# Layer output of a two-layer cross-attention kernel: from four groups of rows to two halves of dimensions, turned back to rows at the layer's end

## The reference, cut to what matters

```python
B, Q, D, H, K, T, F = 8, 56, 256, 16, 128, 1500, 1024
for i in (1, 2):                                   # two layers, both read the same ctx
    h  = layer_norm(x, ln_scale[i], ln_offset[i])
    qh = (h @ wq[i] + bq[i]).reshape(B, Q, H, K)
    kh = (ctx @ wk[i] + bk[i]).reshape(B, T, H, K)  # plus one bias key per head
    vh = (ctx @ wv[i] + bv[i]).reshape(B, T, H, K)  # plus one bias value per head
    weights = softmax(einsum('bqhk,bthk->bhqt', qh, kh) / sqrt(K))
    c  = einsum('bhqt,bthk->bqhk', weights, vh).reshape(B, Q, H * K)
    x  = x + c @ wo[i] + bo[i]                      # "layer output" below
h   = layer_norm(x, ln_mlp_scale, ln_mlp_offset)
out = x + gelu(h @ w_fc1 + b_fc1) @ w_fc2 + b_fc2
```

## Time and profile before

| what | us |
|---|---|
| median of three runs (lowest, highest) | 1249.38 (1248.67, 1249.79) |
| the profiled execution, its own time | 1248.49 |
| its span, first to last instruction | 1246.7 |
| TensorE matmuls busy | 1220.7 (98%) |
| TensorE weight loads busy | 1123.9 (90%) |
| GpSimd busy | 890.2 (71%) |
| VectorE, ScalarE busy | 783.0, 780.1 (63% each) |
| mean granted TensorE clock, share of full speed | 0.999 |

### The profile page before, as it was taken

How to read it: one execution, slowest core, us unless ns; L and a number is a source line. 1 busy time by engine, 2 the same in 40 slices (tenths; PEclk the granted TensorE clock), 3 DMA queues, 4 the chain that set the end, 5 groups by cost and what they waited for, 6 DMA issues and landing times. The chain is left out here.

```text
span 1246.7 us, 26766 instructions
## 1 busy us (share of the span) xinstructions
PE 1220.7 (98%) x7896; PEld 1123.9 (90%) x7896; DVE 783.0 (63%) x1295; ACT 780.1 (63%) x1495; POOL 890.2 (71%) x744
## 2 busy tenths in 40 slices
PE   7999999999999999999999999999999999999998
PEld 6779999999999999998887999999999999999897
DVE  6755666565656565666754666666666666666754
ACT  5756666666666565676584666666666666667665
POOL 4747777777777777678641878686868687866882
PEclk9999999999999999999999999999999999999999
DMA  5401222222222222223320122222222222222321
GB/s 173 130 18 51 56 74 57 71 58 70 61 67 63 66 66 62 57 64 91 110 68 18 38 60 68 62 68 62 67 62 66 63 66 64 65 52 61 74 89 41
DMA packets 147720, 83.60 MB, mean 67 GB/s; under 512 B 121116, under 2 KB 122540, under 8 KB 147672
## 3 DMA queue, kind: packets, MB, share of 16 engines
q1 hardware_dynamic: 147128, 82.27, 25.0%
q10 hardware_dynamic: 544, 0.75, 0.2%
HBM read 68.56 MB, written 0.53 MB: 55 GB/s over the span
## 5 line engine op out<-in xcount | busy, mean ns | idle before, releaser
L602 POOL TENSOR_TENSOR pt<-slots,pt 125x512 fp32r<-125x512 f32 (+3 forms) x384 | 449.5, 1176 | 189.9 <-ACT slots L1067 167.4
L777 PE MATMUL psum<-qs,ctx 128*125 128x384 f32 (+1 forms) x2304 | 534.8, 368 | 1.3 <-ACT slots L1093 0.8
L777 PEld LDWEIGHTS psum<-qs,ctx 128*125 128x125 f32 x2304 | 394.8, 186 | 47.4 <-ACT slots L1093 8.4
L798 PE MATMUL psum<-ctx,pt 125*128 125x258 f32 (+1 forms) x1344 | 385.0, 286 | 5.4 <-ACT on L1074 4.4
L799 PE MATMUL psum<-ctx,pt 125*128 125x256 f32 (+1 forms) x1344 | 379.3, 282 | 0.0
L800 PE MATMUL psum<-ctx,pt 125*128 125x258 f32 (+1 forms) x1344 | 378.6, 282 | 0.0
L1066 ACT ACTIVATE pt<-slots 125x512 fp32r<-125x512 f32 (+3 forms) x384 | 221.6, 577 | 195.6 <-DVE slots L1351 163.6
L1363 DVE TENSOR_TENSOR t_max<-psum,t_max 125x512 f32<-125x512 f32 (+1 forms) x320 | 199.4, 623 | 230.0 <-PE psum L777 230.0
L1093 ACT ACTIVATE slots<-psum 125x512 f32<-125x512 f32 (+1 forms) x384 | 207.5, 541 | 157.6 <-DVE t_max L1363 147.0
L798 PEld LDWEIGHTS psum<-ctx,pt 125*128 125x128 f32 (+1 forms) x1344 | 253.4, 189 | 22.7 <-issue 8.1
L799 PEld LDWEIGHTS psum<-ctx,pt 125*128 125x128 f32 (+1 forms) x1344 | 254.2, 189 | 5.8
(11 more groups left out here) (101 smaller groups left out, 974.4 us busy)
## 6 DMA issues: line engine op xcount, KB each, us to landing
nat_stage<-ctx_nat SPq DMA_DIRECT2D x60, 375.0 KB
tr_stage<-ctx_tr SPq DMA_DIRECT2D x60, 375.0 KB, 3.1
w_raw<-weights SPq DMA_DIRECT2D x70, 256.0 KB, 2.7
qt<-turn SPq DMA_DIRECT2D x256, 32.0 KB, 2.0
qt<-turn SPq DMA_DIRECT2D x224, 24.0 KB, 1.9
dk_rest<-dk_rows SPq DMA_DIRECT2D x2, 768.0 KB, 5.6
w_raw<-weights ACTq DMA_DIRECT2D x2, 256.0 KB, 5.3
dk_first<-dk_rows SPq DMA_DIRECT2D x2, 256.0 KB, 4.2
```

The lines of the kernel that those rows point to most:

```text
L602: nc.gpsimd.tensor_tensor(split_weights(h, LO, c), logits(h, c), as_f32(split_weights(h, HI, c)), ALU.subtract).then_inc(pt_lo, 1)
L777: last = mm(scores(h, k), ctx_tr_chunk(half, a, c), qs[h][:, m, half, 0:R], start=(half, a, m) == terms[0], stop=(half, a, m) == terms[-1])
L798: mm(out_bank[:, 0:D + 2], hi, ctx_nat_hi(c), start=(c == 0), stop=False, skip_group_check=True)
```

## The change

The output of a layer is now accumulated with the dimensions on the partitions: two banks (`YT_BANK`: half 0 in bank 6, half 1 in bank 5), each 128 dimensions x 448 rows. The operands change sides: 128 columns of the output weights are the weights of the array, and `cs` moves, all 448 columns at once. A head takes 2 halves x 3 terms = 6 matmuls. The residual is put there by eight products. At the layer's end half 0 is copied to `ht32` by ScalarE and half 1 by VectorE, TensorE turns both back to rows in `Y_BANK` with eight transposes, and the statistics start from there. Three more filler products stand before the transposes. The MLP keeps the old form.

```diff
@@ tensor @@
             def residual(m):
                 pe.wait_ge(xb_ready, INIT + m * RG + RG)
-                for g in range(RG):
-                    mm(Y_BANK[g][0:RGP, 0:D], ident[0:RGP, 0:RGP], xres[:, g, :], start=True, stop=False)
+                for half in range(DC):
+                    for g in range(RG):
+                        mm(YT_BANK[half][:, g * RGP:(g + 1) * RGP], xres[:, g, half * P:(half + 1) * P],
+                           ident[0:RGP, 0:RGP], start=(g == 0), stop=False)
...
+            def output_half(u, half, last_head):
+                for a, m in TERMS:
+                    last = mm(YT_BANK[half][:, 0:ROWS], w[u][:, m, D + half * P:D + (half + 1) * P], cs[u][:, a, :],
+                              start=False, stop=last_head and (a, m) == (LO, HI))
+                return last
+            def output_cols(u, n):
+                pe.wait_ge(c_lo, INIT + n + 1)
+                for half in range(DC):
+                    last = output_half(u, half, False)
+                last.then_inc(w_used, 1)
+            def last_output_cols(n):
+                pe.wait_ge(c_lo, INIT + n + 1)
+                for half in range(DC):
+                    output_half(2, half, False)
+                pe.wait_ge(c_lo, INIT + n + 2)
+                output_half(3, 0, True).then_inc(yt_mm, 1)
+                output_half(3, 1, True).then_inc(w_used, 2)
+            def turn_back(l):
+                def turned(g, half):
+                    return nc.tensor.transpose(Y_BANK[g][0:RGP, half * P:(half + 1) * P],
+                                               ht32[:, half, g * RGP:(g + 1) * RGP], ident[:])
+                pe.wait_ge(yt_act, INIT + l + 1)
+                for g in range(RG - 1):
+                    turned(g, 0)
+                pe.wait_ge(yt_dve, INIT + l + 1)
+                for g in range(RG - 1):
+                    turned(g, 1).then_inc(rows_mm, 1)
+                turned(RG - 1, 0)
+                turned(RG - 1, 1).then_inc(rows_mm, 1)
...
                 output_quad(heads + 4 * (QUADS - 1), jobs + 4 * (QUADS - 1), True, False, True)
+                keep_busy(3)
+                turn_back(l)
                 keep_busy(15)
                 norm_transposes(l + 1)
@@ scalar @@
                 output_quad(QUADS - 1, False, True)
+                act.wait_ge(yt_mm, INIT + l + 1)
+                go(ht32[:, 0, :], YT_BANK[0][:, 0:ROWS], ACT.Copy).then_inc(yt_act, 1)
                 for g in range(RG):
                     act.wait_ge(xn_ready, INIT + (l + 1) * RG + g + 1)
@@ vector @@
             def output_statistics(m, jobs):
+                dve.wait_ge(w_used, INIT + jobs)
+                V.tensor_copy(ht32[:, 1, :], YT_BANK[1][:, 0:ROWS]).then_inc(yt_dve, 1)
                 for g in range(RG):
-                    rows_complete(m - 1, jobs, g)
+                    dve.wait_ge(rows_mm, INIT + (m - 1) * RG + g + 1)
                     statistics(m, g)
```

More of the change, by code:

```diff
@@ L210, in build @@
         C_BANK = [bank[0], bank[1], bank[7], bank[2]]
+        YT_BANK = [bank[6], bank[5]]
         Y_BANK = [bank[3], bank[4], bank[6], bank[5]]
@@ L248, in build @@
         c_mm, c_hi, c_lo, g32_ready = sem("c_mm"), sem("c_hi"), sem("c_lo"), sem("g32_ready")
-        y_mm, xb_ready, saved, x_ready = sem("y_mm"), sem("xb_ready"), sem("saved"), sem("x_ready")
+        y_mm, yt_mm, yt_act, yt_dve, rows_mm = (
+            sem("y_mm"), sem("yt_mm"), sem("yt_act"), sem("yt_dve"), sem("rows_mm"))
+        xb_ready, saved, x_ready = sem("xb_ready"), sem("saved"), sem("x_ready")
         out_written = sem("out_written")
@@ L260, in build @@
         started_by = {
-            "pe": [w_used, xt_mm, q_mm, qp_mm, lb_mm, s_mm, mt_mm, nb_mm, pv_mm, ot_mm, pn_picked, c_mm, y_mm],
-            "act": [saved, w_hi, h_hi, q_hi, qp_out, most_qs_hi, first_qs_hi, copied, exp_done, on_act, ot_out,
+            "pe": [w_used, xt_mm, q_mm, qp_mm, lb_mm, s_mm, mt_mm, nb_mm, pv_mm, ot_mm, pn_picked, c_mm, y_mm, yt_mm, rows_mm],
+            "act": [saved, yt_act, w_hi, h_hi, q_hi, qp_out, most_qs_hi, first_qs_hi, copied, exp_done, on_act, ot_out,
                     p80_hi, oth_early, oth_hi, c_hi, g32_ready],
@@ L265, in build @@
                     dv_ready, gp_ready, gp_used, q_lo, first_qs_lo, lb_rows_ready, nat_hi, tr_hi, max_done,
-                    max_ready, sub_done, rden_ready, pn_ready, on_dve, ot_last, turned, moved, p80_lo,
+                    max_ready, sub_done, rden_ready, pn_ready, on_dve, yt_dve, ot_last, turned, moved, p80_lo,
                     oth_lo, c_lo, xb_ready],
@@ L871, in output_quad @@
                     if extra and first and u == 0:
-                        output_rows(0, n, False)
+                        output_cols(0, n)
                         head_context(2, n + 2, job + 2, True)
@@ L875, in output_quad @@
                         head_context((u + 2) % 4, n + (u + 2), job + (u + 2), extra)
-                        output_rows(u, n + u, first and u == 0)
-                if last_quad:
+                        if extra:
+                            output_cols(u, n + u)
+                        else:
+                            output_rows(u, n + u, first and u == 0)
+                if last_quad and extra:
+                    last_output_cols(n + 2)
+                elif last_quad:
                     last_output_rows(n + 2)
@@ L1239, in tr_part_hi, with rows_complete @@
                 V.tensor_copy(hi_part, tr_stage[:]).then_inc(tr_hi, 1)
-            def rows_complete(n, jobs, g):
+            def rows_complete(jobs, g):
                 if g < RG - 1:
-                    dve.wait_ge(y_mm, INIT + n * (RG - 1) + g + 1)
+                    dve.wait_ge(y_mm, INIT + g + 1)
                 else:
@@ L1260, in output_sum @@
                 for g in range(RG):
-                    rows_complete(LAYERS, LAYERS * JOBS + FT, g)
+                    rows_complete(LAYERS * JOBS + FT, g)
                     V.tensor_tensor(xres[:, g, :], Y_BANK[g][0:RGP, 0:D], xres[:, g, :], ALU.add).then_inc(x_ready, 1)
```

## The result

The changed kernel takes 1252.32 us (median of nine runs, 1250.15 to 1255.81), the kernel before 1248.67 us beside it (nine runs, 1245.10 to 1249.79). The ratio is 1.0035, with a 95% interval of 1.0024 to 1.0046, so 3.0 to 5.7 us slower. In a second series, with six runs of the changed kernel and 26 of the kernel before, it was 1.0043 (1.0026 to 1.0060). The forecast was +5.05 us, slower.

What follows compares the result with a forecast made beforehand. From head 6 GpSimd and VectorE, not TensorE, were taken to set the output stage's pace. +6.09 (turning back) - 1.16 (last outputs) + 0.12 (residual) - 0 (other outputs) = +5.05 us, on 1249.38 giving 1254.4 us; range 1251.0 to 1256.4.

Steps and rivals of the forecast that it cites:

- Outputs of heads 0 to 12: Output stage: 0.21 us less TensorE time per head, hidden by waiting for GpSimd's weight tile; taken as 0.
- Turns of 2.99 us: Output stage from head 6: `pm`, `oth` and weight tile alternate on GpSimd and VectorE, 2.99 us per head.
- all of it: Upper bound for the earlier outputs: every head's 0.21 us is gained, 2.5 us per layer.
- rival of TensorE's pace: Output stage: TensorE sets the pace, so every output gives its 0.21 us; +0.05 us, 1249.4 us, chance 0.08.
- The last outputs: Last three heads' outputs, with no context between: 36 matmuls become 18, -0.58 us per layer, -1.16 us in all.
- E: The end of a layer's last output matmul, from which the forecast counted the layer's end.
- The residual: Residual put into the output banks: 8 instructions become 16 of 112 columns, +0.06 us per layer, +0.12 us in all.
- Turning back: Layer's end: copies, transposes and unoverlapped statistics delay `ln_v` to E + 4.26, +3.54 and +2.55 us, +6.09 us in all.
- Sum: Whole kernel: all parts together, +5.05 us, slower.
- turning back is cheaper: Rival, layer's end: ScalarE's copy not behind the weight tiles, `ln_v` at E + 3.2; 2.1 us less, 1252.3 us, chance 0.12.
- The clock: Rival, layer's end: idle TensorE is granted 1.2 GHz until the next stage; 1.5 us per layer more, 1257.4 us, chance 0.05.
- The unlocking: Rival, output stage: `oth` precedes `pm`, tile runs alone, 2.64 us per head; total -2.0 us, 1247.4 us, chance 0.05.

Runs made afterwards that it cites:

- extra_matmul: Changed kernel with one more 448-column matmul, its result unread, in the outputs of heads 0 to 13; 1253.36 us, ratio 1.0039 to the kernel before.
- copy_first: Changed kernel with ScalarE's copy of half 0 ahead of its last two weight tiles; 1250.69 us, ratio 1.0016 to the kernel before.
- no_turn_back: Changed kernel without the two copies, three fillers and transposes, so results are wrong; 1249.93 us, ratio 1.0011 to the kernel before.
- pm_on_act_after: Changed kernel with the masked bias product `pm` made by ScalarE instead of GpSimd; 1248.53 us, ratio 1.0000 to the kernel before.
- tile_first_after: Changed kernel with `pm` on ScalarE, half 0 copied before its last two weight tiles, `pm` and tile before `oth`; 1239.09 us, ratio 0.9937.

## Why the prediction was right, step by step

- *Outputs of heads 0 to 12 give nothing.* Right. Turns of 2.99 us in both kernels; extra_matmul put 0.2 us per head back and lost nothing by it. These are 13 outputs, not 12, so the bound "all of it" is 2.7 us per layer and by it the rival of TensorE's pace stands at 1249.0 instead of 1249.4 us. It did not come true at either.
- *The last outputs.* -1.16 us was forecast. From the end of the tile of head 5 to E it is 36.00 us before and 35.36 us after in layer 0, and 35.90 us (from 1179.02) and 35.39 us (from 1182.95) in layer 1: -1.15 us in all.
- *The residual.* +0.12 us was forecast; its 16 instructions take 1.77 us on the chain of layer 1 against 1.73 us, and the first output of either layer starts 0.04 us later behind the residual's start: +0.08 us in all.
- *Turning back.* E + 4.26 was forecast, E + 4.22 came in both layers: +3.50 and +2.51 us, in all +6.01 us for +6.09 us. Of that, copy_first shows 2.3 us to be the copy's place behind the weight tiles; its other part is the turning itself and the overlap that the statistics lost.
- *Sum.* -1.15 + 0.08 + 6.01 = +4.9 us from the trace, inside the 3.0 to 5.7 us of the ratio. The ratio itself gives +4.4 us, the second series +5.4 us; the two medians are 3.65 us apart.
- *What was luck.* The forecast of the time was 1254.4 us, and 1252.32 us came, which is the 1252.3 us of the rival "turning back is cheaper". Of the 2.1 us, 0.7 are that the kernel before took 1248.67 us here and not the 1249.38 us that the forecast started from; the rest is within the interval of the ratio. The absolute time would have spoken for the wrong mechanism, and the ratio hardly speaks against it: that rival stood at +2.95 us, the interval begins at 3.0 us. The rows decide: `ln_v` at E + 4.22 and not E + 3.2, in both profiles of the changed kernel.
- *The rivals.* TensorE's pace is refuted by extra_matmul and no_turn_back. The clock did not fall at the layer's end: windows there show 1.00 (609 to 624 and 1215 to 1230 us). It can fall near there, as no_turn_back shows, and in the second profile of the changed kernel it did once, early in the stage of layer 0 (0.65 in 564 to 568 us). Cheaper turning was refuted by the trace, and copy_first made it true. The unlocking did not happen by itself, and here the working was wrong: it priced a head at 2.64 us once the tile runs alone. In no_turn_back the tile ran alone in 1.28 us, and the pace stayed at 2.99 us. pm_on_act_after took the turn away and got 2.91 us. The 2.64 us needed the weight tile ahead of `oth` too, and then it was 2.66 us.

## What to carry to other kernels

When an engine reads nearly 100% busy, compare the price of one of its groups with the same group elsewhere: 1.47 us against 1.22 us for the same six matmuls was the sign that it waits, since a wait of 0.2 us per head hides in the overlap of matmuls. What it waits for then stands in the timelines of the others. Time saved on an engine that waits in a ring of other engines is idle time, and behind the first limit of such a ring the next can stand within 3%; write down every path of it before pricing what its removal gives. Do not take a forecast as borne out because the time lies in its range: here a rival's time fitted better, and one row (`ln_v` behind the last output) told them apart. And a result that one engine shall pass on quickly has to stand ahead of the work in that engine's list that waits for a later event.

## What the runs showed of the hardware

- VectorE's operation with two inputs from SBUF (`oth`) and GpSimd's do not get on side by side; the later one's record is longer. Where `oth` (1.09 us undisturbed) went first, it had begun 0.2 to 0.7 us earlier, and the tile on GpSimd ended 1.15 us behind its end. Where the tile went first it took 1.27 to 1.30 us and `oth` ended 0.95 us behind it, unless a `pm` came between: 1.43 us long in tile_first_after, where it began 0.82 us behind the tile, and 2.47 us in no_turn_back, where it began while the `pm` ahead of the tile still ran. VectorE's `cs`, with one input in PSUM, took 0.67 to 0.69 us with or without GpSimd beside it.
- Three operations on two engines can hold a turn of one length in two orders: 2.99 us both ways, in the changed kernel and in layer 0 of no_turn_back.
- What lies ahead of the first changed instruction took 556.4 to 559.7 us in the eleven profiles, a scatter nearly as large as the change. The longest had the lowest clock in the first 40 us (0.91), but at 0.96 it was 556.4 to 558.1 us. Differences of a few us are better read from a common instruction on than from whole spans.
- A copy with a scale per partition of 80 x 448 elements took ScalarE 0.66 us; the product of the same size took GpSimd 0.93 us.
